# Sixteen-head attentions of a decoder: a slot for each side product, VectorE on the first keys, the second unit's preparation moved, copies reordered

## The reference

```python
k = (kq @ Wk + bk).reshape(n, T, H, hd_kq).transpose(0, 2, 1, 3)
q = (kq @ Wq + bq).reshape(n, T, H, hd_kq).transpose(0, 2, 1, 3)
vv = (v @ Wv + bv).reshape(n, T, H, hd_v).transpose(0, 2, 1, 3)
scores = jnp.einsum('bhqd,bhkd->bhqk', q, k) + _shifted_causal_mask(T)
attn = jax.nn.softmax(scores, axis=-1)
out = jnp.einsum('bhqk,bhkd->bhqd', attn, vv)
...
h = jax.nn.gelu(out @ W1 + b1, approximate=False)
return h @ W2 + b2
```

## Time and profile before

| what | us |
|---|---|
| median of three executions (1988.14, 1993.07, 1995.74) | 1993.07 |
| span of the profiled execution, first to last instruction | 1991.5 |
| TensorE busy (products) | 1615.1 (81%) |
| VectorE busy | 1231.2 (62%) |
| ScalarE busy | 823.4 (41%) |
| GpSimd busy | 606.1 (30%) |

### The profile page before, as it was taken

The page is one execution under the profiler, slowest core; times in us unless marked ns, Lnnn a source line. Parts: engine busy times, 40 slices in busy tenths (PEclk is TensorE's granted clock), DMA queues, the critical chain, the costliest instruction groups (busy, mean ns, idle before and its releaser), DMA issues. The chain is left out here.

```text
span 1991.5 us, 34855 instructions
## 1 busy us (share of the span) xinstructions
PE 1615.1 (81%) x12400; PEld 1077.5 (54%) x12400; DVE 1231.2 (62%) x4249; ACT 823.4 (41%) x1760; POOL 606.1 (30%) x742
## 2 busy tenths in 40 slices
PE   3378767888779897757988799978877888999888
PEld 1146434454547787644444366745546654677556
DVE  6868645575378999533666333326848875899632
ACT  2232345366227786732344443314643410333422
POOL 4605122430024535304531000022202115777221
PEclk8677877999879999878999898889988987999999
DMA  2000001320036777613321000022210000000000
GB/s 86 0 12 1 10 30 50 83 60 14 7 128 213 262 248 262 219 37 116 84 58 38 18 1 0 1 61 65 62 61 3 1 0 1 2 2 3 2 0 22
DMA packets 81332, 115.59 MB, mean 58 GB/s; under 512 B 8464, under 2 KB 62608, under 8 KB 80400
## 3 DMA queue, kind: packets, MB, share of 16 engines
q0 software_dynamic: 18432, 67.38, 9.7%
q1 hardware_dynamic: 60144, 44.90, 8.1%
q10 hardware_dynamic: 2592, 1.18, 0.3%
HBM read 88.85 MB, written 1.05 MB: 45 GB/s over the span
## 5 line engine op out<-in xcount | busy, mean ns | idle before, releaser
L2643 POOL DMA_INDIRECT f_rows<-tree_table,f_index x128 | 128.8, 1006 | 185.8 <-DVE f_index L2704 75.7
L2844 PE MATMUL f_ps_y<-f_rows,shared_sb 128*128 128x128 f32 x1024 | 129.2, 289 | 31.3 <-ACT f_rows L2916 31.3
L2916 ACT ACTIVATE f_rows<-f_rows,f_low_act 128x128 f32<-128x128 f32 x512 | 153.0, 387 | 0.8
L1667 ACT ACTIVATE x_probs<-x_ps_z 128x768 f32<-128x768 f32 (+1 forms) x128 | 117.4, 917 | 85.6 <-PE x_ps_z L1527 57.6
L82 POOL TENSOR_TENSOR rstd<-moments,shared_sb 128x12 f32<-128x12 f32 (+3 forms) x22 | 4.6, 207 | 480.9 <-DVE moments L66 480.8
L2844 PEld LDWEIGHTS f_ps_y<-f_rows,shared_sb 128*128 128x128 f32 x1024 | 124.5, 203 | 37.2 <-ACT f_rows L2916 33.9
L2743 DVE CUSTOM_DVE_ANT_0 f_rows<-f_rows,f_xn 128x128 f32<-128x128 f32 x512 | 111.3, 287 | 24.2 <-DMA f_rows<-tree_table,f_index 24.2
L1357 DVE TENSOR_REDUCE x_minus_max<-x_ps_s 128x4 f32<-128x1024 f32 x64 | 77.8, 1223 | 73.7 <-PE x_ps_s L1527 73.5
L2095 PE MATMUL f_ps_h<-f_xnT,weights 128*128 128x512 f32 x144 | 76.7, 661 | 2.4 <-ACT f_hT L2160 2.1
L2160 ACT ACTIVATE f_hT<-f_ps_h,weights 128x512 f32<-128x512 f32 x72 | 48.6, 685 | 71.4 <-PE f_ps_h L2095 69.7
L2072 DVE SCALAR_TENSOR_TENSOR x_tokens<-f_ps_y,f_chosen,x_tokens 128x128 f32 (+1 forms) x128 | 36.0, 344 | 67.1 <-PE f_ps_y L2107 67.1
(11 more groups left out here) (661 smaller groups left out, 4191.6 us busy)
## 6 DMA issues: line engine op xcount, KB each, us to landing
x_queries<-x_pieces SPq DMA_DIRECT2D x96, 64.0 KB, 2.1
x_keys<-x_pieces SPq DMA_DIRECT2D x84, 64.0 KB, 2.1
a_queries<-a_pieces SPq DMA_DIRECT2D x48, 64.0 KB, 2.1
weights<-w_L_ffn SPq DMA_DIRECT2D x1, 2953.5 KB, 9.9
a_keys<-a_pieces SPq DMA_DIRECT2D x42, 64.0 KB, 2.1
weights<-w_L_ffn SPq DMA_DIRECT2D x1, 2449.0 KB, 9.7
weights<-w_L_ffn SPq DMA_DIRECT2D x1, 2176.0 KB, 9.2
f_rows<-tree_table,f_index POOLq DMA_INDIRECT x128, 6.1
```

Source lines behind the costliest of these rows:

```text
L1667: a.activation(probs[:, r % HELD, :, :], ps_z[:, :, 0:WIDE], ACT.Exp, scale=scale).then_inc(exped, 1)
L2643: pool.indirect_dma_start(rows[:, place(u, j), tree, :], None, g.tree_table, bass.IndirectOffsetOnAxis(index[:, u % 2, low, j * TREES + tr ...
L2844: last = pe.matmul(ps_y[:, u % SUMS, j, :], g.ident, rows[:, place(u, j), tree, OUT + f * D:OUT + (f + 1) * D], start=False, stop=(low, j, ...
L2916: last = a.activation(row, row, ACT.Copy, scale=low_act[:, u % 3, j * TREES + tree, f:f + 1])
```

## The change

Only `attention16` and its slots are changed.

- Side products get slots of their own. Modulo 8: maxima 0, y 1 (five slots after mix), tokens 2, q 3, mix 4, k 5, v 7; without a tail the addition stands with mix. The second unit's k and v stand in slots 0 and 1, after the first scores.
- The masks are added to `ps_z` right after `shift`, ahead of `score`.
- VectorE normalises the first two units before its loop; the others are GpSimd's, three slots or more ahead of the transposes.
- VectorE splits the first keys; the constants of the stage are prepared after that, and `v_ones` is set in two parts.
- The fills before slot 0 are 2, 1, 8 and 4, in slots -14, -13, -7 and 0. ScalarE takes the second unit's tokens and then issues the first keys' transfers.
- Constant rows of rings 2 and 3 and the clearing of semaphores move from slot -8 to slot 8. The first unit's maxima are turned and split ahead of slot 8's other work.

```diff
--- before.py
+++ after.py
@@ -1160,10 +1160,11 @@
...
     BEHIND = PAIRS + LAG
-    FIRST, LAST = -PAIRS - 7, ALL + BEHIND + PAIRS + 4
+    FIRST, LAST = -PAIRS - 10, ALL + BEHIND + PAIRS + 6
     RINGS, HELD, KEPT = 4, 4, 4
...
     SEEN = ((slice(0, P), slice(STACK, P)), (slice(0, STACK), slice(0, P)))
+    FILLED = {-14: 2, -13: 1, -7: 8, 0: 4}
     with ExitStack() as ctx:
@@ -1204,17 +1205,19 @@
...
         up_made, gelu_ready, mlp_made, mlp_added = (sem(n) for n in ("up_made", "gelu_ready", "mlp_made", "mlp_added"))
-        bias_added = sem("bias_added")
+        bias_added, first_keys_split = sem("bias_added"), sem("first_keys_split")
         block = ctx.enter_context(nc.Block())
...
         pair_at = lambda n: n if 0 <= n < ALL else None
-        norm_in, tokens_in, q_in, k_in, v_in = (lambda slot, early=e: unit_at(slot + early) for e in (15, 14, 13, 12, 10))
+        early = lambda n, second=None: {PAIRS * u - n if u != 1 or second is None else second: u for u in range(UNITS)}
+        norm_in, tokens_in, q_in, k_in, v_in = (
+            early(*e).get for e in ((18,), (14,), (13,), (11, 0), (9, 1)))
         queries_out, keys_out = (lambda slot, early=e: unit_at(slot + early) for e in (11, 8))
...
         weighed_in, sums_in, back_in = (lambda r, late=n: group_in(r, late) for n in (2, 3, 5))
-        mix_in, y_in = (lambda r, late=n: unit_at(r - late) for n in (14, 15))
+        mix_in, y_in = (lambda r, late=n: unit_at(r - late) for n in (16, 21 if tail else 16))
         slots = range(FIRST, LAST)
@@ -1253,11 +1256,11 @@
...
                 sp.dma_start(queries[MAX_ROW::STEP, u % RINGS, :, :], zeros[:, :]).then_inc(stacked[u % RINGS], 16)
+                sp.wait_ge(split, max(2 * u, 1))
+                send(u, 0, queries)
+
+            def stack_keys(u):
                 sp.wait_ge(split, 2 * u + 1)
-                send(u, 0, queries)
-
-            def stack_keys(u):
-                sp.wait_ge(split, 2 * u + 2)
                 send(u, 1, keys)
@@ -1279,7 +1282,9 @@
...
                 if keys_out(slot) == 0:
-                    for ring in range(1, RINGS):
+                    set_constant_rows(1)
+                if maxima_in(slot) == 0:
+                    for ring in range(2, RINGS):
                         set_constant_rows(ring)
@@ -1320,12 +1325,22 @@
...

+            def normalise_unit(u):
+                pool.wait_ge(xT_made, u)
+                for half in range(HALVES):
+                    n = u * HALVES + half
+                    last = pool.tensor_scalar(xn[:, half, :], g.x[:, n, :], g.moments[:, n, 0:1], g.rstd[:, n:n + 1],
+                                              ALU.subtract, ALU.mult)
+                last.then_inc(xn_ready, 1)
+
             for slot in slots:
+                if norm_in(slot) is not None and norm_in(slot) > 1:
+                    normalise_unit(norm_in(slot))
                 if tail and v_in(slot - 1) is not None:
...
                     split_in_three(q_in(slot), 0)
-                if k_in(slot) is not None:
+                if k_in(slot) is not None and k_in(slot) > 0:
                     split_in_three(k_in(slot), 1)
@@ -1335,13 +1350,21 @@
...

-            def normalise_unit(u):
-                v.wait_ge(xT_made, u)
+            def normalise_early(u):
                 for half in range(HALVES):
...
                 last.then_inc(xn_ready, 1)
+
+            def split_first_keys():
+                part = lambda k: pieces[:, 0, 1, k, :]
+                left = rest[:, 1, :]
+                v.wait_ge(k_taken, 1)
+                step(v.tensor_copy(part(0), left))
+                step(v.tensor_tensor(left, left, part(0), ALU.subtract))
+                step(v.tensor_copy(part(1), left))
+                v.tensor_tensor(part(2), left, part(1), ALU.subtract).then_inc(first_keys_split, 1)

@@ -1402,7 +1425,11 @@
...

-            normalise_unit(0)
+            normalise_early(0)
+            v.memset(v_ones[:, 0, :, :, :], 1.0).then_inc(ones_ready, 1)
+            v.wait_ge(xT_made, 1)
+            normalise_early(1)
+            split_first_keys()
             v.wait_ge(g.loaded[name], 16)
@@ -1412,14 +1439,14 @@
...
                 v.tensor_copy(ident16[:, :], g.ident).then_inc(const_ready, 1)
-            v.memset(v_ones[:, :, :, :, :], 1.0).then_inc(ones_ready, 1)
+            v.memset(v_ones[:, 1:KEPT, :, :, :], 1.0).then_inc(ones_ready, 1)
             for slot in slots:
                 r = slot - BEHIND
-                if norm_in(slot) is not None and norm_in(slot) > 0:
-                    normalise_unit(norm_in(slot))
+                if maxima_in(slot) == 0:
+                    split_maxima(0)
                 if pair_at(slot) is not None:
                     take_maxima(slot)
-                if maxima_in(slot) is not None:
+                if maxima_in(slot) is not None and maxima_in(slot) > 0:
                     split_maxima(maxima_in(slot))
@@ -1572,26 +1599,26 @@
...
                 r = slot - BEHIND
-                if slot < 0:
-                    fill_wait(pe, g, ps_s[:, 0, 0, :], 512, 3)
+                if slot in FILLED:
+                    fill_wait(pe, g, ps_s[:, 0, 0, :], 512, FILLED[slot])
                 if slot == 0:
-                    fill_wait(pe, g, ps_s[:, 0, 0, :], 512, 12)
                     pe.wait_ge(const_ready, 1)
+                if maxima_in(slot) == 0:
+                    turn_maxima(0)
                 if PAIRS <= slot <= BEHIND:
...
                     shift(r)
+                    hide(ps_z, r // PAIRS, 1).then_inc(shifted, 1)
                 if pair_at(slot) is not None:
...
                     pe.wait_ge(mask_ready, unit_at(slot) + 1)
-                if pair_at(r) is not None:
-                    hide(ps_z, r // PAIRS, 1).then_inc(shifted, 1)
                 if pair_at(slot) is not None:
...
                     turn_back(back_in(r))
-                if maxima_in(slot) is not None:
+                if maxima_in(slot) is not None and maxima_in(slot) > 0:
                     turn_maxima(maxima_in(slot))
@@ -1646,15 +1673,16 @@
...
                 a.wait_ge((q_made, k_made)[which], u + 1)
-                if u >= 1:
-                    a.wait_ge(split, 2 * u)
+                if u == 1:
+                    a.wait_ge((split, first_keys_split)[which], 1)
+                if u >= 2:
+                    a.wait_ge(split, 2 * u - 2 + which)
                 a.activation(rest[:, which, :], ps_p[:, 0:T], ACT.Identity, bias=w[("q_bias", "k_bias")[which]])\
...
                 a.wait_ge(v_made, u + 1)
-                if u == 0:
-                    a.wait_ge(ones_ready, 1)
+                a.wait_ge(ones_ready, min(u, 1) + 1)
                 if u >= KEPT:
@@ -1680,7 +1708,7 @@
...
             def stack_first_keys():
-                a.wait_ge(split, 2)
+                a.wait_ge(first_keys_split, 1)
                 for slot, of in enumerate(PRODUCTS):
@@ -1700,7 +1728,7 @@
...
                     take_values(v_in(slot))
-                if v_in(slot) == 0:
+                if tokens_in(slot) == 1:
                     stack_first_keys()
```

More of the change, by code:

```diff
@@ L1255, in stack_queries @@
                 sp.dma_start(queries[MAX_ROW::STEP, u % RINGS, :, :], zeros[:, :]).then_inc(stacked[u % RINGS], 16)
-                sp.wait_ge(split, 2 * u + 1)
+                sp.wait_ge(split, max(2 * u, 1))
                 send(u, 0, queries)
             def stack_keys(u):
-                sp.wait_ge(split, 2 * u + 2)
+                sp.wait_ge(split, 2 * u + 1)
                 send(u, 1, keys)
```

## The result

The changed kernel takes 1959.65 us (median of four executions, 1952.63 to 1963.08) against 1990.69 in the same rounds: 0.9835, 95% interval 0.9809 to 0.9861. The profiled execution took 1962.35 with a span of 1960.5, 31.0 less than before (1991.5). In the table entry is the stage's first memset on GpSimd in both kernels (339.91 and 339.82 in x1); before the change it stands 0.04 us ahead of the first fill, which the forecast counts from.

What follows compares the result with a forecast made beforehand. Bound: TensorE's in-order waits on side products sharing one bank, the exponential loop, and slow openings in three stages. 1991.5 - 8.1 - 13.6 - 8.2 - 13 + 1 = 1949.6 of span, median 1951; range 1937 to 1972.

Steps and rivals of the forecast that it cites:

- Part 1 and 3: One side product a slot: 8.1 us first causal, 13.6 masked, 8.2 latent; normalisation from third unit on GpSimd: 0.
- SyncE: ... nothing: Opening: constant rows and semaphore clearing moved behind slot 8's rows and keys, wanted over 12 us later, cost nothing.
- part 2: Hide right behind shift: loop-bound slots gain 0.17 or 0.23 us; about 0.2 a unit, included in part 1's sums.
- Part 4: Openings: fewer fills and earlier first keys save 4 us in first causal, 5 in masked, 4 in latent stage: 13.
- Part 5: Ends: masked stage's last projection, addition and GpSimd's inversion come later, costing 1 us.
- A: Opening gives nothing: slow fills, TensorE at its lower level, second unit's keys late; 1964 us, chance 0.20.
- B: GpSimd's normalisation slow, 2.77 us a call; TensorE waits 1 us at tokens in about ten causal units; 1961, chance 0.11.
- C: TensorE stands at tokens behind GpSimd's normalisation; at 4.0 us a call 3.5 late each, 63 in all; 2014, chance 0.02.
- D: Waits only change place, to VectorE's `divide` in every slot, and reordering moves nothing; about 1991 us, chance 0.03.
- the openings' bound: Openings gain at most 22 us when scores at 16 carry through; range's lower end 1937, chance of more gain 0.04.

Runs made afterwards that it cites:

- e11: Changed kernel with mix and projection back in the slots of tokens and queries: first to last exponential 163.25 us in x2 (changed kernel 155.53), 104.90 in x1 (104.98).
- e3: Changed kernel with the latent stage's (a3) addition one slot later: first to last exponential 102.98 us (changed kernel 104.90).
- e1: Changed kernel with the old order shift, score, masks in all three stages: first to last exponential in x2 150.95 us (changed kernel 155.53).
- e7: Changed kernel with both masks ahead of shift and score in the masked stage: first to last exponential in x2 149.13 us (changed kernel 155.5).
- e4: Changed kernel with unit 1's masks in x2 loaded after the second unit's queries are taken: first scores 16.8 us after entry (19.1), first exponential 41.1 (43.2).
- e6: Changed kernel with first keys issued early, next weights, ring constants and x2's second masks moved later: first exponential 34.7, 38.3, 34.1 us after entry (36.4, 43.2, 35.0).
- e10: Changed kernel with normalisation from the third unit on back on VectorE: slots 1 and 2 together 4.22 us (3.70) in four units of x1 and a3.
- e12: Changed kernel with e7, e3 and e6 combined: 1943.41 us (median of six), ratio 0.9748 to the kernel before.

## Why the prediction was right, and where its sum was off

The time held, and most of the mechanism; the span came 10.9 us above the sum (1960.5 to 1949.6). The reorder in x2 had the wrong sign. Of the signs named in advance, bare back slots (1.41 and 2.05), slots 1 and 2 together (3.70), GpSimd's calls and x1's slot 8 came as said. Others did not: a causal slot of 2.87 (none over 2.3), masked slots of 2.95 (none over 2.8) and units of 21.09 (20.2), and first scores at 19.1 and 15.3 in x2 and a3 (16 to 18).

- **Part 1 and 3, causal.** x1's unit 13.77 (14.1 forecast), slots 1 and 2 together 3.70 (1.41 and 2.29) as forecast, steady -7.5 for -8.1. The wait for unit 1's rows took 1.3; without it the stage would have gained more than forecast, so the near hit is in part luck. "SyncE: ... nothing" was wrong: the transfers were priced by when their data are wanted, not by what is queued behind them on SyncE. That mix's own slot pays was hardly true for x1: 0.4 us for the stage (e11). a3 -5.8 for -8.2: e3 shows 1.7, the addition having moved ahead of a division, which the working never looked at, and the wait for unit 1's rows took 1.3; together a little more than the missing 2.4.
- **Masked stage and part 2.** Steady -7.5 for -13.6, the largest miss. (The terms of its unit add up to 3.42, not 3.5, which is 0.2 over three units.) Part 2 was priced from the loop alone (2.04 against 2.27, and 2.04 or 2.05 came), with nothing for TensorE's own work. e1 gives 4.6 back and e7 6.4; e1's units of 20.1 to 20.3 match the 20.2 forecast, but with the old order. The separation of side products was worth 7.7 (e11).
- **Part 4.** Openings -12.3 for -13, but 4.1, 1.4 and 6.8 for 4, 5 and 4. x1's slot 8 came at 28.6 (27 to 29). That the total came so near is luck in part: the forecast took the fills at 0.45 us each, as the earlier trace rows have them, and "if the clock is at the higher level by then" 16.0; it was at the lower one (0.50), and the first scores came at 16.2 all the same. x2's lost part is unit 1's masks and, beside them, something of the constants, the weights and the late keys on SyncE and ScalarE (e4, e6); a3's 6.8 rests on one profile each side, with a scatter of 3.4 us.
- **Part 5 and the rest.** x2's end +1.7 for +1, x1's -1.7 for 0, other layers +2.0, which is scatter.
- **Rivals.** A is out by the opening's 12.3, though its lower clock came; B and C by 0.79 a call (0.91 at most), D by e10 and e11. B and C reckon with 4.5 us of slack ahead of the tokens, where the working says 5.8. The ends of the range are not quite what their words add up to: 1942 for the openings' bound, 1974 for A and B together. By the Trainium skill, "SBUF — State Buffer", "Who interferes with whom", VectorE's reduces never contend with GpSimd. The trace agrees: most of the calls lie beside reduces and took 0.79. No run puts them beside scans, so the rule itself is not tested here.

## What to carry to other kernels

An order of products on TensorE has a price beside its latency: group products on the same number of array rows, and count the changes per turn before moving one (4.6 to 6.4 us in x2). Two products that share one bank with different readers belong in different slots where the reader is slow (7.7 us in x2, 0.4 in x1). A transfer moved on an in-order queue costs what stands behind it there, so look for the queue's idle gap, and check one turn later whether the wait has come back. Where stages scatter, read an edit from a stretch that repeats: here exponential 8 to the last, within 0.03 us.

## What the runs showed of the hardware

Changing between products on 64 rows and on the full array cost 0.10 us each way, seen in the starts of the products at a granted clock of 1.00. A 128x128 normalisation took 0.79 us on GpSimd in the attention stages (median; 0.91 at most); given back to VectorE, two of them made the slot 0.52 us longer. With fewer fills the granted clock up to x1's first scores was 0.50 to 0.67 in the thirteen runs, and 0.82 in the one profile before; four fills took 1.91 us at the lower level (e6) and 1.03 at the higher one (e12).
